# First cross attention of a decoder: row maxima sent per unit instead of per batch, split on GpSimd, scores three units ahead

## The reference, cut to what matters

```
q = split_heads(Wq x + bq); k = split_heads(Wk c + bk); v = split_heads(Wv c + bv)
q, k = rotary(q), rotary(k)
scores = einsum('bhtc,bhsc->bhts', q, k) / sqrt(16)
p = softmax(scores)
out = Wo einsum('bhts,bhsc->bhtc', p, v) + bo
x = layernorm(x + out)
```

## Time and profile before

| | |
|---|---|
| median of three runs | 3713.44 us |
| the profiled execution | 3739.18 us |
| its span, first to last instruction | 3737.4 us |
| busy in the span: TensorE, VectorE, ScalarE, GpSimd | 84%, 57%, 41%, 22% |
| the phase of the first cross attention | about 624 to 1087 us |

### The profile page before, as it was taken

The page is one execution under the profiler, slowest core; times in us unless marked ns, Lnnn a source line. Parts: engine busy times, 40 slices in busy tenths (PEclk is TensorE's granted clock), DMA queues, the critical chain, the costliest instruction groups (busy, mean ns, idle before and its releaser), DMA issues. The chain is left out here.

```text
span 3737.4 us, 61006 instructions
## 1 busy us (share of the span) xinstructions
PE 3141.4 (84%) x21884; PEld 1811.7 (48%) x21884; DVE 2119.8 (57%) x2654; ACT 1529.9 (41%) x2642; POOL 810.0 (22%) x897
## 2 busy tenths in 40 slices
PE   7888674999949986999996999588888895979986
PEld 4343231333316654888885676122222223757765
DVE  3545444898823554344444344799999961731167
ACT  2221121577743322333331333078888894311121
POOL 3221053022210000110210245201111111151153
PEclk9999886699978997999998999689999997987998
DMA  2000166355431003453543132323333323358975
GB/s 81 27 30 24 38 196 179 88 153 141 126 111 47 29 3 107 127 157 121 153 149 98 51 92 77 92 75 96 100 99 100 97 89 99 112 131 282 388 215 154
DMA packets 383458, 423.79 MB, mean 113 GB/s; under 512 B 69105, under 2 KB 254961, under 8 KB 381954
## 3 DMA queue, kind: packets, MB, share of 16 engines
q1 hardware_dynamic: 221136, 258.92, 22.4%
q10 hardware_dynamic: 140546, 109.08, 9.7%
q0 software_dynamic: 21504, 51.98, 4.6%
HBM read 305.29 MB, written 113.99 MB: 112 GB/s over the span
## 5 line engine op out<-in xcount | busy, mean ns | idle before, releaser
L380 ACT ACTIVATE c_probs<-c_st 128x512 f32<-128x512 f32 x1536 | 834.3, 598 | 308.4 <-PE c_st L308 274.7
L421 DVE TENSOR_REDUCE c_maxes<-c_s 128x2 f32<-128x1024 f32 x768 | 905.2, 1217 | 82.4 <-PE c_s L289 78.1
L325 PE MATMUL c_o<-c_probs,c_v_aug 128*32 128x256 f32 x6144 | 509.2, 404 | 70.1 <-ACT c_o_raw L387 56.6
L289 PE MATMUL c_s<-c_k_st,c_q_st 48*128 48x512 bf16 (+1 forms) x1536 | 359.7, 465 | 116.7 <-DVE c_maxes L421 41.2
L308 PE MATMUL c_st<-c_q_st,c_k_st 51*128 51x512 bf16 (+1 forms) x1536 | 328.8, 404 | 5.2 <-DVE c_y L464 5.1
L289 PEld LDWEIGHTS c_s<-c_k_st,c_q_st 48*128 48x128 bf16 (+1 forms) x1536 | 103.5, 131 | 462.5 <-issue 222.2
L325 PEld LDWEIGHTS c_o<-c_probs,c_v_aug 128*32 128x32 f32 x6144 | 124.0, 109 | 335.6 <-issue 170.2
L308 PEld LDWEIGHTS c_st<-c_q_st,c_k_st 51*128 51x128 bf16 (+1 forms) x1536 | 156.0, 130 | 69.0 <-issue 27.6
L1869 ACT ACTIVATE a_probs<-a_sc 128x512 f32<-128x512 f32 x128 | 66.1, 603 | 281.6 <-PE a_sc L1747 281.6
L3011 DVE TENSOR_TENSOR f_w_lo<-f_w_raw,f_w_hi 128x1536 fp32r<-128x1536 f32 x64 | 117.2, 1831 | 105.0 <-ACT f_w_hi L2932 104.9
L2932 ACT ACTIVATE f_w_hi<-f_w_raw 128x1536 fp32r<-128x1536 f32 x64 | 95.2, 1488 | 89.7 <-PE f_out_ps L2883 62.0
(11 more groups left out here) (405 smaller groups left out, 5920.2 us busy)
## 6 DMA issues: line engine op xcount, KB each, us to landing
c_o_dram<-c_o_raw SPq DMA_DIRECT2D x96, 256.0 KB, 2.3
f_w_raw<-in_f_win ACTq DMA_DIRECT2D x96, 256.0 KB, 3.1
f_w_raw<-in_f_wup ACTq DMA_DIRECT2D x96, 256.0 KB, 3.3
f_w_raw<-in_f_wdown ACTq DMA_DIRECT2D x96, 256.0 KB, 3.5
f_x<-x_dram SPq DMA_DIRECT2D x48, 256.0 KB, 3.9
c_k_dram<-f_parts ACTq DMA_DIRECT2D x96, 128.0 KB, 2.5
c_q_dram<-a_parts SPq DMA_DIRECT2D x96, 128.0 KB, 2.4
c_q_st<-c_q_dram SPq DMA_DIRECT2D x128, 96.0 KB, 2.3
```

The costliest lines, as they stand in the source:

```text
L289: mm = nc.tensor.matmul(s1_ps[:, i, half, :], q_st[r:r + ROWS, s, i, tt * P:(tt + 1) * P], k_st[r:r + ROWS, s, i, :], start=True, stop=True)
L325: mm = nc.tensor.matmul(o_ps[32 * h:32 * h + 32, queries], v_aug[:, (j // NG) % NBS, st, (j % NG) * G + h, :], probs[:, (st * 4 + i * 2 + ...
L380: nc.scalar.activation(probs[:, e % 8, :], st_ps[:, st_bank(j, e), :], ACT.Exp).then_inc(exp_done, 1)
L421: nc.vector.tensor_reduce(maxes[:, jb % 2, :].rearrange("p (h r) -> p h r", h=2)[:, :, c], s1_ps[:, i, :, :], AX.X, ALU.max).then_inc(max_ ...
```

## The change

The first cross attention calls a function of its own, `cross_attention_by_unit`. The second one still calls the old function. The new function is the old one with these differences (for eight heads and this data type):

- VectorE transposes the maxima of each unit at the unit's end (`turn_max`), and rounds nothing. The negation has gone into the constant rows of `c_k_st`.
- GpSimd rounds and takes the remainder for each unit (`split_max`), and issues the store to DRAM. SyncE loads the rows of one unit, with four DMAs per unit in place of four per batch.
- `AHEAD` is 3 in place of 4.
- GpSimd's list is ordered by unit: at g = 0 it splits, normalizes, and fetches the sums and the output; at g = 1 it splits, places v, takes the power, spreads the reciprocals and stores x. What it did for a batch is spread over two.
- On VectorE the statistics, the reciprocal and the last step of the norm stand one maximum later. Behind the last unit the reciprocal of the last batch stands behind the statistics of the one before, and GpSimd sends it off ahead of the store of x.

Old function against new one, cut:

```diff
-    AHEAD = NG + 2
+    AHEAD = 3
-    STEPS = 2 * MP - 1
+    STEPS = 2 * MP - 2
-    ONES = TWO_ONES if dt == BF16 else 1.0
+    MINUS = TWO_MINUS_ONES if dt == BF16 else -1.0
...
-                def send_max(b, j0):
+                def send_max(it, j):
 
-                    sp.wait_ge(m_step, (b + 1) * STEPS)
-                    sp.sem_inc(passed_sp, 1)
-                    sp.dma_start(m_dram[bass.ds(b, 1), :, :, :].rearrange("o p m c -> p (o m) c"),
-                                 m_parts[:, (j0 // NG) % 2, :, :].bitcast(plain)).then_inc(m_stored, 16)
-                    s0 = j0 % RING
-                    sp.wait_ge(m_stored, 16 * (b + 1))
+                    u = it * RING + j
+                    sp.wait_ge(m_stored[j % 2], 16 * (it * (RING // 2) + j // 2 + 1))
+                    if begun(u - 1):
+                        sp.wait_ge(st_full, (u - 2) * EXPS + 1)
...
-                        if g == NG - 2 and unit_exists(j + 2, last):
-                            send_max(b + 1, j + 2)
+                        if unit_exists(j + AHEAD - 1, last):
+                            send_max(it, j + AHEAD - 1)
...
                     if st == 0 and i == 0:
-                        pe.wait_ge(m_ld, 32 * MP * (it * NBS + j // NG + 1))
+                        pe.wait_ge(m_ld[j % 2], 32 * MP * (it * (RING // 2) + j // 2 + 1))
...
+                def turn_max(it, j):
+
+                    u = (it + j // RING) * RING + j % RING
+                    dve.wait_ge(max_done, 2 * KT * (u + 1))
+                    if begun(u - 1):
+                        dve.wait_ge(m_step, (u - 1) * STEPS)
+                    nc.vector.transpose(m_t[:, j % 2, :], maxes[:, j % 2, :]).then_inc(m_turned, 1)
...
+                def split_max(it, j):
+
+                    u = it * RING + j
+                    out, whole = m_parts[:, j % 2, :, :], m_t[:, j % 2, :]
+                    pool.wait_ge(m_turned, u + 1)
+                    if begun(u - 1):
+                        pool.wait_ge(m_ld[j % 2], 32 * MP * (it * (RING // 2) + j // 2))
+                    pool.sem_inc(passed_pool, 1)
+                    nc.gpsimd.tensor_copy(out[:, 0, :], whole).then_inc(m_step, 1)
+                    pool.wait_ge(m_step, u * STEPS + 1)
+                    pool.sem_inc(passed_pool, 1)
+                    rest = m_rest[:, :] if MP == 3 else out[:, 1, :]
+                    nc.gpsimd.tensor_tensor(rest, whole, out[:, 0, :], ALU.subtract).then_inc(m_step, 1)
...
+                    pool.dma_start(m_dram[bass.ds(u, 1), :, :, :].rearrange("o p m c -> p (o m) c"),
+                                   out.bitcast(plain)).then_inc(m_stored[j % 2], 16)
...
                 rounds(pool, body)
-                gather_o(UNITS // RING - 1, NBS - 1)
                 if PROJ:
-                    power(B - 2)
-                    store_x(B - 2, 0)
+                    normalize(B - 2, B - 2, B // 2 - 1)
+                gather_o(UNITS // RING - 1, NBS - 1)
+                power(B - 2)
+                spread_recip(B - 1)
+                store_x(B - 2, 0)
                 normalize(B - 1, B - 1, B // 2 - 1)
```

More of the change, by code:

```diff
@@ L17 @@
 TWO_ONES = 1.0 + 2.0 ** -9 - 2.0 ** -16
+TWO_MINUS_ONES = -(1.0 + 0xBF80 / 2 ** 23)
 class Phase:
@@ L3877, in decoder @@
             i["c0_cos"], i["c0_sin"], i["c0_bqk"], i["c0_bv"])
-    cross_attention(nc, "c0", 8, x1, q, k, v, x2, i["half"], F32R, i["c0_wo"], i["c0_bo"])
+    cross_attention_by_unit(nc, "c0", 8, x1, q, k, v, x2, i["half"], F32R, i["c0_wo"], i["c0_bo"])
     q1, k1 = dram("c1_q", (B, 16, 48, D), BF16), dram("c1_k", (B, 16, 48, D), BF16)
```

470 lines of the change are left out of this document (added).

## The result

| | runs | median us | lowest to highest |
|---|---|---|---|
| before | 5 | 3706.49 | 3697.43 to 3716.21 |
| after | 5 | 3681.25 | 3677.04 to 3698.07 |

The account below looks back on a forecast made before the run. VectorE was taken to bound the start, TensorE to lead narrowly in the middle. The terms -9.0 + 1.0 + 0 + 0 - 4.2 = -12.2 us gave 3701 us from a median of 3713.44, range 3684 to 3720.

Parts of the forecast that it names:

- The start: Ahead of the first exponential: three units ahead in place of four bring the first transposed scores 9.0 us sooner.
- Unit 28: In the loop: it now holds scores for unit 31, taking 11.5 us in place of 10.5, 1.0 us lost.
- The road of the maxima: From VectorE over GpSimd, DRAM and SyncE to TensorE: maxima sent by unit arrive in time, new wait 0.
- the sum of the road: Steps and DMAs from a unit's maxima to their landing: 7.4 us at best, 9.8 as taken, 16.8 at worst.
- VectorE's idle 0.88 us: In a middle batch: VectorE idles 0.88 us twice ahead of the residual, which hides the new transposes, cost nothing.
- The end: Behind the last unit: the last reciprocals go out at once, not behind the earlier power and store; 4.2 us gained.
- That jump stays in the program: In the loop: the 4.02 us wait, behind which TensorE fell to the low clock, was to remain.
- I assume the same stretch again: Behind the first transposed scores: TensorE stays at 1.2 GHz for 40.8 us as before, costing 17.4 us.
- the clock rises early: Rival, first cross attention's start: low clock lasts 8 us instead of 41, 14 us less, 3687 us; chance 0.13.
- The sum: Over the first cross attention: -9.0 + 1.0 + 0 + 0 - 4.2 = -12.2 us, giving 3701 us.
- The offset: Whole kernel: the profiled execution lay 25.7 us above the runs' median 3713.44; terms were carried over to that median.

Follow-up runs that it names:

- e5: The kernel before with three units of scores ahead in place of four in the first cross attention: 3703.31 us, ratio 0.9986.
- e6: The changed kernel with four units of scores ahead in place of three, maxima still sent three units ahead: 3720.81 us, ratio 1.0017.
- e7: The kernel before with the new order behind the last unit, last reciprocals sent ahead of the store of x: 3712.01 us, ratio 0.999.
- e2: The changed kernel once more, no edit, against the kernel before: 3705.37 us, ratio 0.997.
- e9: The changed kernel, unaltered, once more beside its shifted copy: 3711.94 us, ratio 0.9978 to the kernel before.
- e13: The changed kernel with 32 matmuls of 32x32 (64 instructions) added in the second cross attention: 3673.68 us, ratio 0.9894 to the kernel before.
- e15: The kernel before with three units ahead and 32 matmuls of 32x32 added in the second cross attention: 3668.96 us, ratio 0.9882.
- e16: The changed kernel, unaltered, compared on the same chip with the kernel before: 3692.14 us, ratio 0.9942.
- e3: The kernel before with one 128x128 matmul added behind each block of scores ahead of the loop: 3725.32 us, ratio 1.0018.
- e10: The changed kernel with 16 matmuls of 32x32 (64 instructions) added ahead of the first exponential: 3682.86 us, ratio 0.9907 to the kernel before.
- e4: The changed kernel with one 128x128 matmul added behind each block of scores ahead of the loop: 3698.4 us, ratio 0.9959 to the kernel before.
- e14: The kernel before with 32 matmuls of 32x32 added in the second cross attention: 3691.88 us, ratio 0.9937.
- e11: The kernel before with 16 matmuls of 32x32 (64 instructions) added ahead of the first cross attention's first exponential: 3690.13 us, ratio 0.9925.

## Why the prediction was wrong, point by point

**The start: right.** Forecast -9.0, measured -8.6 to the first transposed scores (-9.2 from the first maximum); 27.34 us behind the first maximum where 27.5 was forecast. e5 and e6 show that the number of units ahead does this alone.

**Unit 28: right**, +0.7 for +1.0.

**The road of the maxima: right at 0.** No wait for it, the batch 22.93 us, copies 3 to 14 within 0.2 us. That the two steps on GpSimd with the waits behind them take 1.36 us, not 0.8, stayed inside the room that the sum of the road had left. One reading under it was off: VectorE's idle 0.88 us stands ahead of the residual once a batch, not twice.

**The end: right in kind, too large.** Forecast -4.2, measured -3.5 to the last store of x, since 0.63 us remain between the reciprocals and their store, and only -1.5 to the next phase. e7 keeps the whole gain with the old function, so the 2.1 us behind the last store are the new function's. Its expectation names more semaphores to clear in the closing barrier; that was not tried.

Two steps failed, and both are terms that were put at nothing: the wait at the loop's jump and the low clock at the start.

**"That jump stays in the program": wrong.** The 4.02 us of the earlier trace rows were read as a property of the loop; they go with where TensorE's instructions lie, and with whether the loop's instructions are loaded again. The change has 32 instructions less ahead of the loop, and the wait is gone in all seven traces with three units ahead and no matmuls added ahead of this loop (after, e2, e5, e9, e13, e15, e16), and there in all eleven others. From copy 14 to copy 17 the seven take 39.2 us on the mean. The eleven, e3 with its longer low clock left out, take 43.6. That is a further term of -4.4 us, with the clock's share in it: two of the seven (e2, e5) stayed at 2.4 GHz and took 35.4 and 35.8 us, the other five fell to 1.2 GHz for 6.8 to 17.1 us even without the wait and took 38.2 to 41.6.

**"I assume the same stretch again": wrong for this execution**, and a wrong kind of assumption. In the two profiled executions it is the larger miss: 13.6 us to the copy of unit 3. The rival "the clock rises early" had priced it at 14 us and given it a chance of 0.13. The low clock after the first transposed scores lasted 6 us in the profile of after, and in that of e10, with the same start, it lasted 40.8 us:

```profile
664.21 0.66 PE L882 MATMUL c_st<-c_q_st,c_k_st 50*128 50x512 f32 x2
...
702.88 0.79 PE L863 MATMUL c_s<-c_k_st,c_q_st 48*128 48x512 f32 x2
...
704.98 0.50 PE L863 MATMUL c_s<-c_k_st,c_q_st 48*128 48x512 f32 x2
```

From the first transposed scores to the copy of unit 3 nine executions with three units ahead took 48.8 us on the mean (45.6 to 59.2), seven with four ahead 54.7 (48.3 to 61.9), e3 and e4 left out. So a shorter start may bring the rise earlier, by some 6 us; with standard errors of 1.4 and 2.0 this is likely, not shown. The Trainium skill (TensorE: Matmul & The Clock Gate, Part 1: The HAM clock gate) has sustained matmuls at the full clock within a few microseconds: the 6 us agree with it, the 41 us do not, and both are executions of the same pattern of steps.

**The sum again**, with what was learned: -8.6 - 4.4 + 0.7 - 1.5 = -13.8 us that the traces bear out, and perhaps -6 us for the clock: -20 us. e13 against e14, the change with the second loop free in both, is -18.8 us on the means, twice the standard error 6.6, and fits either. For the unaltered kernels the four comparisons (after, e2, e9, e16) gave, on the means, -22, -11, -6 and -24 us; their mean is -16 us, and -13 weighed by the numbers of runs. So the forecast of -12.2 us is near what the change brings over all its runs, and that is in part luck, since it holds nothing for the jump and a larger term for the end. Of the 25 us in the first comparison some 5 to 11 were luck of the clock in untouched stages, the last sublayer above all, if the profiled execution stands for the others. What stays open is why the comparisons differ as they do, by more than their own scatter: the waits at the jumps were the same in all four, and the two stages that scatter most were seen in one profile each.

**The offset** of the profile (25.7 us above the median) was carried over as if it were work. It was scatter too: before's own runs spread from 3692 to 3749 us.

## What to carry to other kernels

Here a wait for "issue" at a hardware loop's jump went with the place of the code and not with its work: before believing a gain or a loss of a few us in a kernel with such loops, compare the stages that the edit did not touch, count these waits and the packets of the instruction queues, and try the kernel with a few idle matmuls ahead of the loop. Here that was worth 19 us without any change to the work, as much as the whole change. Where single runs scatter by 12 us, judge an edit by stretches between landmarks in two traces or more of either kernel, and its time by ten runs or more.

## What the runs showed of the hardware that was not expected

- Shifting TensorE's instructions by 64 took five waits of 3 us out of a loop's jumps; shifting them by 128 brought them back, at 4 us. In the second cross attention the unit at a jump takes 13.0 to 14.7 us with a wait of 3 us and 15.3 to 15.8 with one of 4, in place of 10.4.
- A loop with the wait loads nine packets of 16 KB on the instruction queue in each iteration, a loop without it none: 192, 183, 147 or 138 packets in all, by which of the two loops has it.
- The 64 instructions may lie in the sublayer concerned or three sublayers ahead of it: the effect is the same (the second cross attention takes 736.6 and 734.4 us in e10 and e11, and 736.6 us in e13).
- 24 and 32 matmuls of 128x128 between the first scores, on an engine that was at 1.2 GHz and waited for VectorE, did not raise the granted clock.
- On GpSimd a cast of 128x64 takes 0.24 us and a subtraction 0.32 us, but the waits of the following instruction for each are 0.18 and 0.63 us (`after`, at 996 us).
